# Weight maxima dealt 3, 2, 2, 1 and squares 2, 1, 1 over the first attention steps, and one root and one reciprocal for two batches in the last stage

## The chip, the cores and the metric

The kernel runs as one launch on one core of one Trainium2 chip. The metric is the device time of the launch in microseconds (us). Three timed runs of the kernel before gave 409.97, 409.61 and 407.93 us, so the median is 409.61 us. The engines are named as in the profile: PE is TensorE's matmul, PEld its weight load, DVE is VectorE, ACT is ScalarE, POOL is GpSimd, and SP is SyncE, which here only issues DMAs.

## What is computed

16 batches of 256 tokens with 128 channels go through a block with adaptive layer norm: causal linear attention with 16 heads of 8, then a mixture of 8 experts of which each token takes two. Cut to what matters here:

```python
h = _layernorm(x) * (1 + ca) + sa
x = x + ga * linear_attention(h)                 # cumulative sums of k (x) v, 16 heads
h = rmsnorm((_layernorm(x) * (1 + cb) + sb) @ W_in.T, in_norm_w)
gates = softmax over the two best of (h @ Wr.T + expert_bias)
for e in range(8):
    oe = (silu(h @ Wg[e].T) * (h @ Wu[e].T)) @ Wd[e].T
    out = out + gates[:, e:e + 1] * rmsnorm(oe, enorm_w[e])
x = x + gb * (rmsnorm(out, out_norm_w) @ W_out.T)
```

## The kernel before

A token sits on one of 128 partitions, and a batch is two tiles of 128 tokens. Every engine has its own program in a written order, and the engines meet only in semaphores. The kernel has three stages.

**Attention and routing** is a pipeline of steps. In step s one batch is normalized (`nrm`, batch s), the one before it is projected to q, k and v (`qkv`), and batches s-2 to s-5 are in the running state (`att`), the output projection (`prj`), the way into the experts (`inp`) and the routing (`rte`). Steps 0 to 7 are written out and use only the batches that exist: `inp` begins in step 4 and `rte` in step 5. Steps 8 and later are a loop. Between two steps nothing synchronizes all engines; each goes on as its waits allow. On DVE a step begins with `den` (L1130) and ends with `weights(s)`; on ACT a step ends with the deviation `sd2` of the second layer norm (L665), the squares of the routing and the second normalization `xn2`.

Work on the expert weights is put into these steps. They are loaded by SP early on: `wguT` (4 MB) into `late`, then `wd` (2 MB) and `enorm` (0.5 MB), the last two counted by `moe_ld`. Their scales have to be known before the expert stage. DVE takes the maximum of |wgu| in eight chunks of 1024 columns (`wmaxs`, L1089): two chunks at the end of each of steps 3, 4, 5 and 6, that is `MAX_STEPS`. At the end of step 6 it joins them (L1094 to L1097), and in step 7 (`SCALE_STEP`) the scale goes through PE and comes back (`weight_power`, `weight_scale`, L1108 to L1119). ACT takes sums of squares of `wd` in four chunks of 1024 columns (L739): two in step 6 and two in step 7, that is `SQUARE_STEPS`. In an ACT step they stand between the first normalization (`xn`, L631) and `sd2` (L665). DVE waits for `sd2` in `norm_inv` (L909), ahead of its `weights(s)`.

**The experts** are tiles of 256 rows of one expert each, paced by PE. The change does not touch them.

**The combination** mixes the two expert rows of every token, normalizes the mix, multiplies by `W_out` and adds x, a batch at a time. For a batch b: POOL makes `half` (L603); DVE adds the other half, `mix_experts` (L1422, two instructions); PE transposes the mix (L1872); ACT takes its sum of squares (`norm_out`, L867, two instructions), copies the transposed mix to `mixT` (L873) and takes the root `rms5` (L874); PE multiplies (L1880); DVE takes the reciprocal `rinv5` (`rms_out`, L1429) and writes the output `ob` (`add_out`, L1438, two instructions); SP stores it. On DVE the order of a turn is: reciprocal of batch b-2, mix of batch b, output of batch b-2. Batches 0 to 7 are written out, and their loads from DRAM come in the groups of `LOADS`, each with a root and coefficients of its own (L859, L1411, L1413). Batches 8 to 15 are a loop of two rounds with four batches each.

Of the kernel before, what the change touches and what calls it, by code (L numbers as in the profile page):

```python
# [100 lines left out]
def block_kernel(nc, x, c_wmod, weights_all, qkv_b, out_b, e_bias, wguT, wdT, e_norm, consts, place, filler, out):  # L101
    ctx = ExitStack()
    with ctx:
        def sb(name, shape, dt=F32):
            return ctx.enter_context(nc.sbuf_tensor(name, shape, dt))
# [164 lines left out]
        ob = kv[:, 0].rearrange("p t s -> p (t s)")[:, 0:4 * L].rearrange("p (j t d) -> p j t d", j=4, t=NT)  # L270
        mixT = mixT.rearrange("p j t d -> p j (t d)")
        rms4, rinv4, coef = (sb(n, [P, B * NT, K]) for n in ("rms4", "rinv4", "coef"))
        ssq4 = sb("ssq4", [P, 2, NT])
        rms5 = sb("rms5", [P, 2, NT])
        rinv5 = sb("rinv5", [P, 2, NT])

        bk = [ctx.enter_context(nc.psum_tensor(f"bank{i}", [P, 512], F32)) for i in range(8)]

# [343 lines left out]
        def _(act):  # L622
# [53 lines left out]
            def step(nrm, qkv, att, prj, inp, rte):  # L676
# [54 lines left out]
                    w = bass.ds(nrm[0] * WC - (SCALE_STEP + 1) * WC, WC)  # L731
                    nc.scalar.activation(w_hi[:, w], wgu[:, w], ACT.Copy, scale=w_by[:]).then_inc(whi_done, 1)
                s = nrm[0] if nrm is not None else B
                if isinstance(s, int) and s in SQUARE_STEPS:

                    if s == SQUARE_STEPS[0]:
                        act.wait_ge(moe_ld, 32)
                    for c in range(2 * (s - SQUARE_STEPS[0]), 2 * (s - SQUARE_STEPS[0]) + 2):
                        nc.scalar.activation(wd_junk, wd[:, c * DC:(c + 1) * DC], ACT.Square,  # L739
                                             accum_out=wd_sq[:, c:c + 1]).then_inc(wdsq_done, 1)  # L740
                        act.wait_ge(wdsq_done, c + 1)
# [117 lines left out]
                nc.scalar.activation(rms4[:, w], yb[:, w, :, D], ACT.Sqrt, bias=eps_rms[:],  # L859
                                     scale=1.0 / D).then_inc(rms4_done, 1)  # L860

            def norm_out(b, p, n):
                act.wait_ge(mix_done, b + 1)
                if again(n):
                    act.wait_ge(rinv5_done, b - 1)
                for t in range(NT):
                    nc.scalar.activation(junk[:], mix[:, p, t, :], ACT.Square,  # L867
                                         accum_out=ssq4[:, p, t:t + 1]).then_inc(ssq4_done, 1)
                    act.wait_ge(ssq4_done, NT * b + t + 1)
                act.wait_ge(mixT_ps, b + 1)  # L870
                if again(n):
                    act.wait_ge(o_ps, b - 1)
                nc.scalar.activation(mixT[:, p, :], bk[p][:, 0:L], ACT.Copy).then_inc(mixT_done, 1)  # L873
                nc.scalar.activation(rms5[:, p, :], ssq4[:, p, :], ACT.Sqrt, bias=eps_rms[:],  # L874
                                     scale=1.0 / D).then_inc(rms5_done, 1)

            rms_of_rows(0)
            rms_of_rows(1)
            for b in range(8):
                norm_out(*batch_of_turn(0, b))  # L880
                if b in (0, 1, 5):
                    rms_of_rows((0, 1, 5).index(b) + 2)
            with act.Fori(2, B // 4) as i:
                for j in range(4):
                    norm_out(*batch_of_turn(i, j))


        @block.vector
        def _(dve):
# [190 lines left out]

            def weights(s):

                if isinstance(s, int) and s in MAX_STEPS:

                    if s == MAX_STEPS[0]:
                        dve.wait_ge(wgu_ld, 16)
                    n = WN // len(MAX_STEPS)
                    for c in range((s - MAX_STEPS[0]) * n, (s - MAX_STEPS[0] + 1) * n):
                        nc.vector.tensor_reduce(wmaxs[:, c:c + 1], wgu[:, c * WC:(c + 1) * WC], AX.X, ALU.max,  # L1089
                                                apply_absolute_value=True).then_inc(wmaxs_done, 1)  # L1090
                    if s == MAX_STEPS[-1]:
# [324 lines left out]
            def mix_experts(b, p, n):  # L1416
                dve.wait_ge(half_done, b + 1)
                if again(n):
                    dve.wait_ge(mixT_ps, b - 1)
                    dve.wait_ge(ssq4_done, NT * (b - 1))  # L1420
                for t in range(NT):
                    last = nc.vector.scalar_tensor_tensor(  # L1422
                        mix[:, p, t, :], yb_of(b, t, 1), coef[:, bass.ds(b * NT + t, 1), 1],
                        half[:, p, t, :], ALU.mult, ALU.add)
                last.then_inc(mix_done, 1)

            def rms_out(b, p, n):
                dve.wait_ge(rms5_done, b + 1)
                nc.vector.reciprocal(rinv5[:, p, :], rms5[:, p, :]).then_inc(rinv5_done, 1)  # L1429

            def add_out(i, j):
                b, p, _ = batch_of_turn(i, j)
                dve.wait_ge(rinv5_done, b + 1)
                dve.wait_ge(o_ps, b + 1)
                if not (isinstance(b, int) and b < 4):
                    dve.wait_ge(stored[j % 4], 16 * (i + j // 4))
                for t in range(NT):
                    last = nc.vector.scalar_tensor_tensor(  # L1438
                        ob[:, j % 4, t, :], bk[2 + p][:, t * D:(t + 1) * D], rinv5[:, p, t:t + 1],
                        x_all[:, bass.ds(b * L + t * P, P)], ALU.mult, ALU.add)  # L1440
                last.then_inc(ob_done, 1)

# [498 lines left out]
```

## Time and profile before

| | |
|---|---|
| median of the timed runs | 409.61 us |
| all timed runs | 409.97, 409.61, 407.93 us |
| profiled execution, its own time | 404.05 us |
| profiled execution, span of the core | 402.2 us |
| busy share of the span | PE 94%, DVE 81%, ACT 73%, POOL 60% |
| steps 3 to 7 of the attention stage | 23.6 to 78.5 us |
| combination | 371 to 402 us |

The span is what the trace covers; the remaining 1.85 us of the execution's own time lie around it. Places in the trace are given as us from the start of the span.

### The profile page before, as it was taken

The numbers are of one execution on the slowest core, as the hardware profiler recorded it, in microseconds if no ns is written. First come the engines' busy times: TensorE is split into PE (matmuls) and PEld (weight loads), VectorE is DVE, ScalarE is ACT, GpSimd is POOL, SyncE is SP. The second block draws the span as 40 slices with busy tenths as digits, with TensorE's granted clock in tenths as the row PEclk, the third lists the DMA queues.
The fourth block names the chain that finished last, engine by engine and source line by source line (L and its number), as shares of the span: only waits on it lengthen the run. The fifth ranks groups of instructions, "written<-read, shape, count | busy, mean of one in ns | idle before, by whom it ended". The sixth has DMA issues, their size and how long they took to land.

```text
span 402.2 us, 13139 instructions
## 1 busy us (share of the span) xinstructions
PE 376.7 (94%) x3890; PEld 315.5 (78%) x3891; DVE 324.2 (81%) x1040; ACT 292.0 (73%) x817; POOL 239.7 (60%) x211
## 2 busy tenths in 40 slices
PE   8899998999999999999799999999999999999764
PEld 4788886888888888885379989999989899984443
DVE  5568998899999999886979878777878777871786
ACT  5455767877778888646478777878778778874685
POOL 0665587678888888875544545555555545553341
PEclk9999999999999999999999999999999999999999
DMA  7999973647464330011134332323232333213933
GB/s 223 365 358 405 315 238 113 225 132 221 145 200 168 131 131 26 29 48 39 48 69 59 70 68 58 76 55 71 61 79 53 61 70 60 60 42 111 356 100 91
DMA packets 47380, 52.60 MB, mean 131 GB/s; under 512 B 34675, under 2 KB 40710, under 8 KB 44518
## 3 DMA queue, kind: packets, MB, share of 16 engines
q1 hardware_dynamic: 42806, 42.84, 35.3%
q0 software_dynamic: 4544, 9.39, 7.8%
q8 instruction: 16, 0.26, 0.3%
q14 instruction: 14, 0.11, 0.1%
HBM read 35.73 MB, written 30.38 MB: 164 GB/s over the span
## 4 chain that ended last, share of the span: by engine, by line
PE 69%; DVE 10%; issue 6%; ACT 6%; DMA 5%; POOL 3%; DVEq 0%; SPq 0%; ACTq 0%; POOLq 0%
PE bank L1512 11%; PE bank L1784 9%; PE bank L1788 8%; PE bank L1787 8%; PE bank L1592 4%; PE bank L1803 4%; PE bank L1805 4%; PE bank L1804 4%; PE bank L1535 3%; DVE prod L992 2%; ACT junk L867 2%; DVE wmaxs L1089 1%; DMA dispatched<-filler 1%; PE bank L1649 1%; PE bank L1599 1%
## 5 line engine op out<-in xcount | busy, mean ns | idle before, releaser
L583 POOL DMA_INDIRECT expert_rows<-late,to_place x74 | 78.1, 1056 | 75.2 <-DVE late L1365 63.2
L1784 PE MATMUL bank<-late,w_hi 128*128 128x256 f16 x312 | 85.1, 273 | 1.9 <-issue 1.2
L532 POOL TENSOR_TENSOR kv<-kv,v 128x1024 f32<-128x1024 f32 x32 | 67.7, 2133 | 29.9 <-ACT kv L716 29.7
L1788 PE MATMUL bank<-late,w_lo 128*128 128x256 f16 x312 | 85.1, 273 | 0.0
L1787 PE MATMUL bank<-late,w_hi 128*128 128x256 f16 x312 | 85.1, 273 | 0.0
L1351 DVE SCALAR_TENSOR_TENSOR kv<-bank,uscale,kv 128x512 f32<-128x512 f32 x78 | 58.4, 750 | 26.6 <-ACT kv L801 23.2
L550 POOL DMA_INDIRECT dispatched<-rows,pos x60 | 63.8, 1063 | 23.2 <-issue 17.6
L1512 PE MATMUL bank<-cst,kv 128*128 128x128 f32 x576 | 73.5, 278 | 1.0 <-DVE den L1130 1.0
L1512 PEld LDWEIGHTS bank<-cst,kv 128*128 128x128 f32 x576 | 68.1, 192 | 1.5 <-issue 1.5
L801 ACT ACTIVATE kv<-bank,descale 128x512 f32<-128x512 f32 x78 | 53.5, 687 | 13.1 <-PE bank L1788 9.2
L807 ACT ACTIVATE kv<-kv 128x512 f16<-128x512 f32 x78 | 48.8, 626 | 17.5 <-DVE kv L1351 14.7
L1358 DVE TENSOR_TENSOR kv<-kv 128x512 f16<-128x512 f32 x78 | 54.5, 700 | 5.3 <-ACT kv L807 3.7
L1804 PE MATMUL bank<-late,kv 128*128 x304 | 52.9, 219 | 0.0
L1803 PE MATMUL bank<-late,kv 128*128 x304 | 52.9, 219 | 0.0
L1805 PE MATMUL bank<-late,kv 128*128 x304 | 52.9, 219 | 0.0
L992 DVE TENSOR_TENSOR prod<-bank,qT 128x384 f32<-128x384 f32 x96 | 49.6, 544 | 0.0
L1784 PEld LDWEIGHTS bank<-late,w_hi 128*128 x312 | 30.4, 98 | 6.7 <-issue 3.4
L1788 PEld LDWEIGHTS bank<-late,w_lo 128*128 x312 | 30.5, 98 | 3.7
L1787 PEld LDWEIGHTS bank<-late,w_hi 128*128 x312 | 30.5, 98 | 3.1
L1662 PE MATMUL bank<-ones 128*128 128x512 bf16 x129 | 29.5, 379 | 1.7 <-DMA dispatched<-rows,pos 1.7
L1804 PEld LDWEIGHTS bank<-late,kv 128*128 128x128 f16 x304 | 29.7, 98 | 0.4
L631 ACT ACTIVATE xn<-x_all,nmr,rs 128x128 f32<-128x128 f32 (+1 forms) x64 | 27.8, 482 | 3.0 <-DVE nmr L914 2.9
(248 smaller groups left out, 787.2 us busy)
## 6 DMA issues: line engine op xcount, KB each, us to landing
dispatched<-filler SPq DMA_DIRECT2D x17, 1032.0 KB
late<-wguT SPq DMA_DIRECT2D x1, 4096.0 KB, 18.0
late<-expert_rows SPq DMA_DIRECT2D x1, 2064.0 KB, 12.6
gates_bc<-gate_rows SPq DMA_DIRECT2D x1, 2048.0 KB, 7.2
wd<-wdT SPq DMA_DIRECT2D x1, 2048.0 KB, 25.2
out<-kv SPq DMA_DIRECT2D x16, 128.0 KB, 1.8
expert_rows<-late,to_place POOLq DMA_INDIRECT x78
late<-expert_rows SPq DMA_DIRECT2D x1, 1032.0 KB, 7.9
```

The costliest lines, as they stand in the source:

```text
L532: nc.gpsimd.tensor_tensor(kvt[:, 0:HD, :, :], k_in, v_in.to_broadcast([P, HD, H, HD]), ALU.mult).then_inc(kv_done[t], 1)
L550: pool.indirect_dma_start(hbuf, bass.IndirectOffsetOnAxis(ap=pos[:, p, t * K + k:t * K + k + 1], axis=0), rows[:, p, t, k, :], None).then_ ...
L583: pool.indirect_dma_start(ybuf, bass.IndirectOffsetOnAxis(ap=to_place[:, s, r:r + 1], axis=0), yt[:, s, r, :], None).then_inc(y_scat[s], 16)
L992: nc.vector.tensor_tensor(prod[:, t, cc * THIRD * P:(cc + 1) * THIRD * P].rearrange("p (e i) -> p e i", i=P), cum, qT[:, p, t * P:(t + 1) ...
L1351: nc.vector.scalar_tensor_tensor(gu[:, h, :], U[h], uscale[:], sg[:, h, :], ALU.mult, ALU.mult).then_inc(gu_done, 1)
L1512: last = mm(CUM[cc][:, j * P:(j + 1) * P], kv[:, p, t, e * D:(e + 1) * D], tri, start=True, stop=True)
L1784: mm(o, wh, hi, start=True, stop=False)
L1787: mm(o, wh, lo, start=False, stop=False)
L1788: last = mm(o, wl, hi, start=False, stop=True)
L1803: mm(o, gu_hi[:, s % 2, h, g], wh, start=(f == 0 and (apart or r == 0)), stop=False)
L1804: mm(o, gu_lo[:, s % 2, h, g], wh, start=False, stop=False)
L1805: last = mm(o, gu_hi[:, s % 2, h, g], wl, start=False, stop=(f == FC - 1 and (apart or r == RB - 1)))
```

## The change

Three tables of work are dealt anew.

- The eight chunks of the maxima (`MAX_CHUNKS`) go three to step 3, two to step 4, two to step 5 and one to step 6. Joining them stays at the end of step 6.
- The four chunks of the squares (`SQUARE_CHUNKS`) go two to step 4, one to step 6 and one to step 7. The wait for `moe_ld` goes with the first of them, to step 4.
- In the combination the sums of squares of two batches stand side by side (`ssq4`, `rms5` and `rinv5` have four batch slots), and ACT takes one root (L876 after the change) after the odd batch. DVE takes one reciprocal (L1431 after it) for both, and it stands behind the mix of the next even batch, no longer ahead of it. The two outputs that need it follow.

```diff
-        MAX_STEPS = range(SCALE_STEP - 4, SCALE_STEP)
+        MAX_CHUNKS = {SCALE_STEP - 4: range(0, 3), SCALE_STEP - 3: range(3, 5), SCALE_STEP - 2: range(5, 7),
+                      SCALE_STEP - 1: range(7, WN)}
-        SQUARE_STEPS = range(B - WN - DN // 2, B - WN)
+        SQUARE_CHUNKS = {SCALE_STEP - 3: range(0, 2), SCALE_STEP - 1: range(2, 3), SCALE_STEP: range(3, DN)}
...
-            def norm_out(b, p, n):
+            def norm_out(i, j):
...
                 nc.scalar.activation(mixT[:, p, :], bk[p][:, 0:L], ACT.Copy).then_inc(mixT_done, 1)
-                nc.scalar.activation(rms5[:, p, :], ssq4[:, p, :], ACT.Sqrt, bias=eps_rms[:],
-                                     scale=1.0 / D).then_inc(rms5_done, 1)
+                if j % 2:
+
+                    if again_turn(i):
+                        act.wait_ge(rinv5_done, 2 * i + j // 2 - 1)
+                    nc.scalar.activation(rms5[:, j - 1:j + 1, :], ssq4[:, j - 1:j + 1, :], ACT.Sqrt, bias=eps_rms[:],
+                                         scale=1.0 / D).then_inc(rms5_done, 1)
...
-            def rms_out(b, p, n):
-                dve.wait_ge(rms5_done, b + 1)
-                nc.vector.reciprocal(rinv5[:, p, :], rms5[:, p, :]).then_inc(rinv5_done, 1)
+            def rms_out(i, j):
+                pair, slots = 2 * i + j // 2, slice(j % 4, j % 4 + 2)
+                dve.wait_ge(rms5_done, pair + 1)
+                nc.vector.reciprocal(rinv5[:, slots, :], rms5[:, slots, :]).then_inc(rinv5_done, 1)
...
                 for j in batches:
-                    before = batch_of_turn(i, j - 2)
-                    rms_out(*before)
                     mix_experts(*batch_of_turn(i, j))
+                    if j % 2 == 0:
+                        rms_out(i, j - 2)
                     add_out(i, j - 2)
...
+            rms_out(0, B - 2)
             for b in (B - 2, B - 1):
-                rms_out(*batch_of_turn(0, b))
                 add_out(0, b)
```

On ACT, in step 4 of the attention stage, the program before has these rows (`q_raw`, `qT`: the query; `xn` is the first and `xn2` the second normalized input; `sd2` is what DVE waits for):

```order
L723 ACTIVATE q_raw<-bank3,small 128x256
L725 ACTIVATE qT<-q_raw,eps_f 128x256
L631 ACTIVATE xn<-x_all,nmr,rs 128x128 x2
L665 ACTIVATE sd2<-mv2,eps_ln 128x2
L670 ACTIVATE junk,ssq<-bank7 128x128 x2
```

The changed program has at the same place:

```order
L722 ACTIVATE q_raw<-bank3,small 128x256
L724 ACTIVATE qT<-q_raw,eps_f 128x256
L630 ACTIVATE xn<-x_all,nmr,rs 128x128 x2
L738 ACTIVATE w_lo,wd_sq<-wd 128x1024 x2
L664 ACTIVATE sd2<-mv2,eps_ln 128x2
L669 ACTIVATE junk,ssq<-bank7 128x128 x2
```

Two squares of `wd` now stand ahead of `sd2` in step 4. In step 6 and in step 7 one square stands there where two did.

On DVE, in the loop of the combination, a turn of an even batch reads before (`prod` is the mix, `kv` the output, `bank2` and `bank3` the products of the even and the odd batch, ISA and REGISTER_ALU are register work):

```order
L1429 RECIPROCAL rinv5<-rms5 128x2
L1417 REGISTER_ALU
L1422 ISA x2
L1422 SCALAR_TENSOR_TENSOR prod<-late,coef,prod 128x128
L1422 ISA x2
L1422 SCALAR_TENSOR_TENSOR prod<-late,coef,prod 128x128
L1436 REGISTER_ALU
L1438 ISA
L1438 SCALAR_TENSOR_TENSOR kv<-bank2,rinv5,x_all 128x128
L1438 ISA
L1438 SCALAR_TENSOR_TENSOR kv<-bank2,rinv5,x_all 128x128
```

In the changed program it reads:

```order
L1423 ISA x2
L1423 SCALAR_TENSOR_TENSOR prod<-late,coef,prod 128x128
L1423 ISA x2
L1423 SCALAR_TENSOR_TENSOR prod<-late,coef,prod 128x128
L1430 REGISTER_ALU
L1431 RECIPROCAL rinv5<-rms5 128x4
L1438 REGISTER_ALU
L1440 ISA
L1440 SCALAR_TENSOR_TENSOR kv<-bank2,rinv5,x_all 128x128
L1440 ISA
L1440 SCALAR_TENSOR_TENSOR kv<-bank2,rinv5,x_all 128x128
```

The reciprocal moved from ahead of the mix to between the mix and the first output that needs it, and it now covers four columns: it needs the root that ACT takes after the odd batch of the pair. The turn of an odd batch has no reciprocal any more.

## Rows read from the trace of the kernel before

**Rows 1.** The page: busy time by engine, and the chain by engine.

```profile
PE 376.7 (94%) x3890; PEld 315.5 (78%) x3891; DVE 324.2 (81%) x1040; ACT 292.0 (73%) x817; POOL 239.7 (60%) x211
...
PE 69%; DVE 10%; issue 6%; ACT 6%; DMA 5%; POOL 3%; DVEq 0%; SPq 0%; ACTq 0%; POOLq 0%
```

**Rows 2.** Steps 4, 6, 8: us, busy PE PEld DVE ACT POOL, clock, DMA share, GB/s.

```profile
33.88:43.80 9.92, 9.66 (x106) 8.58 (x105) 8.75 (x32) 6.57 (x20) 5.46 (x4) 1.00 1.01 397
...
54.64:67.28 12.64, 11.25 (x117) 9.37 (x115) 11.11 (x49) 9.58 (x27) 9.76 (x8) 1.00 0.47 153
...
78.47:88.80 10.33, 10.04 (x108) 8.42 (x107) 9.80 (x44) 8.33 (x24) 8.00 (x7) 1.00 0.43 133
```

**Rows 3.** Timeline of DVE, steps 4, 6 and 7: start, us, instruction, [idle before].

```profile
41.10 0.15 DVE L909 RECIPROCAL rs<-sd 128x2 f32<-128x2 f32 x1
...
41.55 2.33 DVE L1089 TENSOR_REDUCE wmaxs<-late 128x1 f32<-128x1024 f32 x2
...
63.77 0.17 DVE L909 RECIPROCAL rs<-sd 128x2 f32<-128x2 f32 x1 [0.76 <-ACT sd L665]
...
76.29 0.17 DVE L909 RECIPROCAL rs<-sd 128x2 f32<-128x2 f32 x1 [0.46 <-ACT sd L665]
...
77.69 0.16 DVE L1116 COPY wpow<-bank 128x1 f32<-128x1 f32 x1 [0.63 <-PE bank L1658]
```

**Rows 4.** Timeline of ACT, steps 4 and 6.

```profile
39.33 0.86 ACT L631 ACTIVATE xn<-x_all,nmr,rs 128x128 f32<-128x128 f32 x2
40.09 0.28 ACT L665 ACTIVATE sd<-mv,eps_ln 128x2 f32<-128x2 f32 x1
...
62.25 1.06 ACT L739 ACTIVATE w_lo<-wd 128x1024 f16<-128x1024 f32 x1
...
63.44 0.30 ACT L665 ACTIVATE sd<-mv,eps_ln 128x2 f32<-128x2 f32 x1
```

**Rows 5.** Timeline of SP: the issue of the load of `enorm`.

```profile
29.87 0.43 SPq L416 DMA_DIRECT2D enorm<-e_norm  x1
```

**Rows 6.** DMA issues: KB, and median us from issue to landing.

```profile
enorm<-e_norm SPq DMA_DIRECT2D x1, 512.0 KB, 10.0
```

**Rows 7.** Timeline of ACT in the combination: first root of loads, batches 8 to 12.

```profile
370.88 0.30 ACT L859 ACTIVATE rms<-late,eps_rms 128x4 f32<-128x4 f32 x1 [5.16 <-DMA late<-expert_rows]
...
388.44 0.29 ACT L874 ACTIVATE rms<-ssq,eps_rms 128x2 f32<-128x2 f32 x1
388.62 0.30 ACT L867 ACTIVATE junk<-prod 128x128 f32<-128x128 f32 x1
...
389.48 0.38 ACT L873 ACTIVATE prod<-bank 128x256 f32<-128x256 f32 x1
389.75 0.29 ACT L874 ACTIVATE rms<-ssq,eps_rms 128x2 f32<-128x2 f32 x1
...
392.40 0.29 ACT L874 ACTIVATE rms<-ssq,eps_rms 128x2 f32<-128x2 f32 x1
393.07 0.31 ACT L867 ACTIVATE junk<-prod 128x128 f32<-128x128 f32 x1 [0.39 <-DVE prod L1422]
```

**Rows 8.** Timeline of DVE in the combination.

```profile
371.28 0.18 DVE L1411 RECIPROCAL rinv<-rms 128x4 f32<-128x4 f32 x1 [7.96 <-ACT rms L859]
371.50 0.16 DVE L1413 TENSOR_TENSOR coef<-rinv,gate_all 128x4 f32<-128x4 f32 x1
...
384.00 0.35 DVE L1411 RECIPROCAL rinv<-rms 128x32 f32<-128x32 f32 x1 [0.29 <-ACT rms L859]
...
389.00 0.15 DVE L1429 RECIPROCAL rinv<-rms 128x2 f32<-128x2 f32 x1
389.20 0.62 DVE L1422 SCALAR_TENSOR_TENSOR prod<-late,coef,prod 128x128 f32<-128x128 f32 x2
389.79 0.61 DVE L1438 SCALAR_TENSOR_TENSOR kv<-bank,rinv,x_all 128x128 f32<-128x128 f32 x2
390.31 0.15 DVE L1429 RECIPROCAL rinv<-rms 128x2 f32<-128x2 f32 x1
```

More of the change, by code:

```diff
@@ L272, in block_kernel @@
         rms4, rinv4, coef = (sb(n, [P, B * NT, K]) for n in ("rms4", "rinv4", "coef"))
-        ssq4 = sb("ssq4", [P, 2, NT])
-        rms5 = sb("rms5", [P, 2, NT])
-        rinv5 = sb("rinv5", [P, 2, NT])
+        ssq4, rms5, rinv5 = (sb(n, [P, 4, NT]) for n in ("ssq4", "rms5", "rinv5"))
         bk = [ctx.enter_context(nc.psum_tensor(f"bank{i}", [P, 512], F32)) for i in range(8)]
@@ L733, in step @@
                 s = nrm[0] if nrm is not None else B
-                if isinstance(s, int) and s in SQUARE_STEPS:
-                    if s == SQUARE_STEPS[0]:
+                if isinstance(s, int) and s in SQUARE_CHUNKS:
+                    if SQUARE_CHUNKS[s][0] == 0:
                         act.wait_ge(moe_ld, 32)
-                    for c in range(2 * (s - SQUARE_STEPS[0]), 2 * (s - SQUARE_STEPS[0]) + 2):
+                    for c in SQUARE_CHUNKS[s]:
                         nc.scalar.activation(wd_junk, wd[:, c * DC:(c + 1) * DC], ACT.Square,
@@ L860, in rms_of_rows @@
                                      scale=1.0 / D).then_inc(rms4_done, 1)
-            def norm_out(b, p, n):
+            def norm_out(i, j):
+                b, p, n = batch_of_turn(i, j)
                 act.wait_ge(mix_done, b + 1)
-                if again(n):
-                    act.wait_ge(rinv5_done, b - 1)
                 for t in range(NT):
                     nc.scalar.activation(junk[:], mix[:, p, t, :], ACT.Square,
-                                         accum_out=ssq4[:, p, t:t + 1]).then_inc(ssq4_done, 1)
+                                         accum_out=ssq4[:, j, t:t + 1]).then_inc(ssq4_done, 1)
                     act.wait_ge(ssq4_done, NT * b + t + 1)
@@ L879, in _ @@
             for b in range(8):
-                norm_out(*batch_of_turn(0, b))
+                norm_out(b // 4, b % 4)
                 if b in (0, 1, 5):
@@ L884, in _ @@
                 for j in range(4):
-                    norm_out(*batch_of_turn(i, j))
+                    norm_out(i, j)
         @block.vector
@@ L1081, in weights @@
             def weights(s):
-                if isinstance(s, int) and s in MAX_STEPS:
-                    if s == MAX_STEPS[0]:
+                if isinstance(s, int) and s in MAX_CHUNKS:
+                    if MAX_CHUNKS[s][0] == 0:
                         dve.wait_ge(wgu_ld, 16)
-                    n = WN // len(MAX_STEPS)
-                    for c in range((s - MAX_STEPS[0]) * n, (s - MAX_STEPS[0] + 1) * n):
+                    for c in MAX_CHUNKS[s]:
                         nc.vector.tensor_reduce(wmaxs[:, c:c + 1], wgu[:, c * WC:(c + 1) * WC], AX.X, ALU.max,
                                                 apply_absolute_value=True).then_inc(wmaxs_done, 1)
-                    if s == MAX_STEPS[-1]:
+                    if MAX_CHUNKS[s][-1] == WN - 1:
                         dve.wait_ge(wmaxs_done, WN)
@@ L1425, in mix_experts @@
                 last.then_inc(mix_done, 1)
-            def rms_out(b, p, n):
-                dve.wait_ge(rms5_done, b + 1)
-                nc.vector.reciprocal(rinv5[:, p, :], rms5[:, p, :]).then_inc(rinv5_done, 1)
+            def rms_out(i, j):
+                pair, slots = 2 * i + j // 2, slice(j % 4, j % 4 + 2)
+                dve.wait_ge(rms5_done, pair + 1)
+                nc.vector.reciprocal(rinv5[:, slots, :], rms5[:, slots, :]).then_inc(rinv5_done, 1)
             def add_out(i, j):
                 b, p, _ = batch_of_turn(i, j)
-                dve.wait_ge(rinv5_done, b + 1)
+                dve.wait_ge(rinv5_done, 2 * i + j // 2 + 1)
                 dve.wait_ge(o_ps, b + 1)
@@ L1438, in add_out @@
                     last = nc.vector.scalar_tensor_tensor(
-                        ob[:, j % 4, t, :], bk[2 + p][:, t * D:(t + 1) * D], rinv5[:, p, t:t + 1],
+                        ob[:, j % 4, t, :], bk[2 + p][:, t * D:(t + 1) * D], rinv5[:, j % 4, t:t + 1],
                         x_all[:, bass.ds(b * L + t * P, P)], ALU.mult, ALU.add)
```

## The prediction

> **What bounds the kernel now.** I read the page first: PE is busy for 94% of the span and holds 69% of the chain that ended last [rows 1]. The change takes nothing from PE, so only the places where PE itself waits for DVE or ACT can move the time. Next I read the busy time by stretch, a step of the attention stage to each row. In the loop a step takes 10.33 us and PE is busy for 10.04 of it: there PE paces, and work on DVE or ACT is hidden. Step 6 takes 12.64 us with PE busy for 11.25 of it, so 1.4 us without work on PE, and with DVE busy for 11.11 [rows 2]. In the steps that carry the maxima DVE's end sets the next step's start: the next batch's statistics stand behind the maxima on DVE, then come ACT's `sd` and `hT`, then PE. Then the timelines of DVE and ACT, to see where DVE itself waits. In steps 6 and 7 it waits 0.76 and 0.46 us for ACT's `sd2`, in step 4 not at all [rows 3]. In the combination ACT works back to back, 1.32 us to a batch, and DVE 1.31 [rows 7, 8]: a stage in which two engines pass batches to and fro at nearly the same pace, with PE mostly idle. These two stretches are all that the change touches, and both lie on the path.
>
> **Maxima.** Two chunks take from 41.55 to the start of step 5 at 43.80, so one costs 1.13 us of DVE [rows 2, 3]. DVE has no idle time ahead of them in step 3, so the third chunk makes step 3 1.13 longer: **+1.1**. Steps 4 and 5 keep two. Step 6 loses one: **-1.1**, as long as something else doesn't end later there. What is left of step 6 is 12.64 - 1.13 - 0.76 (next part) = 10.75 us, still above the 10.33 at which PE paces a step, so the whole of it is given back. The maxima alone come to nothing.
>
> **Squares.** One square takes 1.19 us of ACT, from 62.25 to the `sd2` at 63.44 [rows 4]. In step 4 `sd2` starts at 40.09 right behind `xn`. With two squares between them it starts at 40.09 + 2.38 = 42.47, and DVE's reciprocal follows 0.33 later, as in step 6 (63.44 to 63.77): at 42.80. Before, it stood at 41.10 with no wait. DVE is late by **1.7 us** there [rows 3, 4]. Behind this wait on DVE are the shift of the norm, the two maxima and all of step 5, so nothing absorbs it: step 5 starts 1.7 later. The cover that the squares had in steps 6 and 7 was routing work on DVE, which in step 4 has not begun. In step 6 one square fewer brings `sd2` forward by 1.19, more than the wait of 0.76: **-0.8**. In step 7 the wait of 0.46 also goes, but DVE then waits 0.63 for PE at 77.69, and PE had been busy without a gap up to there [rows 3]: the scale comes when PE delivers it, so **0**. The loads: ACT now asks for `moe_ld` in step 4, at 40.1 + 1.1 = 41.2. `enorm`, the later of the two, is issued at 29.87 and lands 10.0 later, at 39.9 [rows 5, 6]. It is there, with 1.3 us to spare. The first stage sums to +1.1 - 1.1 + 1.7 - 0.8 = **+0.9**. Bounds: if the late `sd2` is wholly hidden, -0.8; if the gain in step 6 fails, +1.7.
>
> **Root and reciprocal.** A root takes 0.18 us of ACT's pace (388.44 to 388.62) and a reciprocal 0.1 to 0.2 of DVE's [rows 7, 8]. Eight of each go. Alone that would give ACT 0.18 per pair of batches. But the reciprocal for both batches needs the root after the odd one, and it now stands ahead of both outputs and of every later mix. DVE's loop becomes a ring, which I add up in instructions of this trace, from the root of an odd batch to that of the next. Root to reciprocal 0.40 (370.88 to 371.28); reciprocal to the output that reads it 0.22 (371.28 to 371.50); output to the next mix 0.52 (389.79 to 390.31) and 0.1 for the register work; the mix 0.62 (389.20); 0.1 to hand it to ACT (the 0.40 above less the root's own 0.30); squares 0.86 (388.62 to 389.48); copy 0.27 (to 389.75) [rows 7, 8]. That is 3.09 us for a pair. Before, it took 392.40 - 389.75 = 2.65 [rows 7]. The old ring held one batch: root, reciprocal, mix, squares and copy give 0.40 + 0.20 + 0.62 + 0.1 + 1.13 = 2.45 for two batches, just under ACT's 2.65, so it didn't show.
>
> How many pairs pay? The roots after batches 1 and 3 come before DVE asks for them, since the loads and halves pace that part. From batch 5 on: DVE asks for the root of pair (4, 5) ahead of coefficients 4 (384.00) [rows 8]; the ring makes these, and so the mix of batch 7, late by some 0.3. Pair (8, 9) comes by the ring plus the loop's entry, +0.1. Pair (10, 11) pays 3.09 - 2.65 = 0.45. At the loop's turn ACT waited 0.39 for DVE already [rows 7], so (12, 13) pays about 0.2. Pair (14, 15) pays 0.45 again. The sum is **+1.5**. Bounds: below, no wait at all and eight roots saved, 8 x 0.18 = -1.4; above, all seven passages from pair to pair pay 0.45, +3.1. I take 1.5, worked from the ring with the waits that the trace has.
>
> The rule weighed against this: the Trainium skill, "Perfetto Trace Analysis", section "Optimizing Scalar/DVE Operations", says that grouping small operations of Scalar and DVE helps when the engine is saturated. ACT is, in this loop, and by the rule alone the stage would gain the -1.4 of the lower bound. The same section says that breaking work up may let it complete sooner when the wait is elsewhere, and that is how I read the ring. The rule's gain is the first rival.
>
> **The sum.** +0.9 + 1.5 = +2.4 us on the profiled execution: 404.05 to 406.5. Its own time is 5.6 below the median of the timed runs; I carry the difference over, 409.61 + 2.4 = **412.0**.
>
> **The rivals.**
>
> 1. *Grouping pays* (15%): not slower. The place is the reciprocal behind the even mix. If ACT's root is there when DVE's mix ends, ACT paces and the stage loses 1.4; with +0.9 that is 409.1. It decides at the mix: its end would have to come 0.40 after the root's start or later. For it: DVE's own pace is 1.31 and it often comes late. Against: ACT starts the root at 389.75, DVE would be free at 389.79 and the root lands at 390.15 [rows 7, 8].
> 2. *The squares hide in step 4* (12%). DVE or PE is late there for another reason, and only -0.8 remains of the first stage: 409.6 - 0.8 + 1.5 = 410.3. Against it: DVE shows no wait at 41.10.
> 3. *Both of these* (5%): 409.6 - 0.8 - 1.4 = 407.4.
> 4. *The loads come late* (10%). If `enorm` lands beyond 41.2, each further us stands on ACT, then on DVE. Three us late is 1.7 more: 413.7. For it: the DMA engines are full in step 4 (share 1.01) [rows 2], and the timed runs take 5.6 us longer than this trace.
> 5. *The ring is shorter than I add it* (13%): hand-overs overlap, and the last stage costs 0.5: 411.0.
>
> **How the numbers follow.** The forecast has 45%, with a range of its own from 411.0 to 413.2. A measurement of this kernel tells about 0.5% from no change, 2.05 us, so slower begins at 411.66. Two thirds of the forecast lie there, and rival 4, and little of 5 and of the spread of the runs (the three before span 0.5%): 46%. Faster is rival 3 and the tail of 1: 7%. The rest, 47%, is within. The range from 408.9 to 413.9 leaves out rival 3 and the ends of 4 and of the spread.
>
> **What would show it.** In step 4 of the changed kernel DVE waits some 1.6 us for `sd2` at L909's place, in steps 6 and 7 not at all, and step 5 starts near 46.6 instead of 43.80. Step 3 is 1.1 longer, step 6 is 10.7 to 10.8. The loop from step 8 on is unchanged but starts 0.9 later. In the combination DVE waits 0.3 to 0.6 for the root at every even batch from 6 on, ACT waits for DVE at the odd batches, and two batches take 3.1. It is wrong if DVE's reciprocal never waits, if step 4 keeps 9.9 us, or if ACT stands at the first square for the load.

## The result and the profile after

The changed kernel takes 410.68 us (median of 9 runs, 409.20 to 412.01) against 409.61 for the kernel before (9 runs beside it, 406.57 to 411.55). The ratio is 1.0064, with a 95% interval of 1.0033 to 1.0096: 2.6 us slower, between 1.4 and 3.9. The two medians differ by only 1.07; the ratio compares runs taken side by side, so I go by it.

The page of the changed kernel, busy time by engine and the chain by engine (before: [rows 1]):

```profile
span 408.1 us, 13116 instructions
...
PE 379.5 (93%) x3890; PEld 317.7 (78%) x3891; DVE 323.7 (79%) x1032; ACT 291.4 (71%) x809; POOL 239.7 (59%) x211
...
PE 58%; DVE 18%; issue 8%; ACT 6%; DMA 4%; POOL 3%; DVEq 1%; SPq 0%; ACTq 0%; POOLq 0%
```

Eight instructions fewer on DVE and on ACT, as the change says, and their busy times are lower by 0.5 and 0.6. The chain runs over DVE for 18% of the span, where it was 10%. That is 33 us more, far beyond what the change costs, and the traces of its two halves below have 12% (e1) and 10% (e2): this share is no measure of the change.

The profiled span grew from 402.2 to 408.1, by 5.9, more than the timed runs did. I cut both traces at the same instructions (the `den` of each step; the first root of the loads in the combination; the end):

| stretch | before | after | difference |
|---|---|---|---|
| ahead of step 3 | 23.63 | 26.23 | +2.60 |
| step 3 | 10.25 | 11.38 | +1.13 |
| step 4 | 9.92 | 11.59 | +1.67 |
| step 5 | 10.84 | 10.85 | 0 |
| step 6 | 12.64 | 10.67 | -1.97 |
| step 7 | 11.19 | 11.18 | 0 |
| step 8 to the combination | 292.41 | 292.40 | 0 |
| combination | 31.32 | 33.80 | +2.48 |

The first row is no effect of the change, which has nothing there: over the traces of this study this stretch takes anything from 23.63 to 27.38, for kernels that are the same up to it. What lies in the parts that the change touches is +0.83 and +2.48, together 3.3, inside the interval. The stretch from step 8 to the combination, which it doesn't touch, takes from 291.94 to 293.03 over the same traces, so its agreement to 0.01 here is chance.

Busy time by stretch of the changed kernel, steps 4, 6 and 7 (columns as in [rows 2]):

```profile
37.61:49.20 11.59, 10.18 (x104) 8.67 (x104) 8.84 (x31) 8.76 (x24) 5.47 (x3) 1.00 0.84 311
...
60.05:70.72 10.67, 9.98 (x108) 8.35 (x107) 9.97 (x48) 8.43 (x25) 8.94 (x7) 1.00 0.40 129
70.72:81.90 11.18, 11.12 (x118) 9.55 (x117) 9.44 (x50) 8.43 (x25) 8.13 (x8) 1.00 0.62 199
```

Step 4 is longer by 1.67 with DVE as busy as before (8.84) and 1.4 us without work on PE. The clock is 1.00 in all of them.

Timeline of DVE, the same steps (before: [rows 3]), then of ACT in step 4 (before: [rows 4]):

```profile
46.50 0.17 DVE L911 RECIPROCAL rs<-sd 128x2 f32<-128x2 f32 x1 [1.58 <-ACT sd L664]
...
46.95 2.33 DVE L1090 TENSOR_REDUCE wmaxs<-late 128x1 f32<-128x1024 f32 x2
49.20 0.18 DVE L1131 TENSOR_SCALAR den<-bank 128x32 f32<-128x32 f32 x1
...
68.34 0.16 DVE L911 RECIPROCAL rs<-sd 128x2 f32<-128x2 f32 x1
...
69.01 1.21 DVE L1090 TENSOR_REDUCE wmaxs<-late 128x1 f32<-128x1024 f32 x1
...
79.19 0.14 DVE L911 RECIPROCAL rs<-sd 128x2 f32<-128x2 f32 x1
...
81.12 0.16 DVE L1117 COPY wpow<-bank 128x1 f32<-128x1 f32 x1 [1.18 <-PE bank L1660]
```

```profile
43.06 0.86 ACT L630 ACTIVATE xn<-x_all,nmr,rs 128x128 f32<-128x128 f32 x2
43.83 1.04 ACT L738 ACTIVATE w_lo<-wd 128x1024 f16<-128x1024 f32 x1
44.99 1.06 ACT L738 ACTIVATE w_lo<-wd 128x1024 f16<-128x1024 f32 x1
46.17 0.29 ACT L664 ACTIVATE sd<-mv,eps_ln 128x2 f32<-128x2 f32 x1
```

ACT goes from `xn` into the first square without a gap, so the loads had landed. `sd2` comes two squares later (46.17 - 43.83 = 2.34 us), DVE waits 1.58 for it, and the two maxima and step 5 stand behind that wait. In step 6 the wait of 0.76 is gone (68.34). In step 7 the wait for `sd2` (0.46) is gone too (79.19), and the one for PE grew from 0.63 to 1.18: the step stayed as long as it was.

Timeline of DVE in the combination (before: [rows 8]), then of ACT (before: [rows 7]). The first two rows of DVE lie ahead of the loop, the last two behind it:

```profile
387.56 0.18 DVE L1431 RECIPROCAL rinv<-rms 128x4 f32<-128x4 f32 x1 [0.40 <-ACT rms L876]
387.77 0.61 DVE L1440 SCALAR_TENSOR_TENSOR kv<-bank,rinv,x_all 128x128 f32<-128x128 f32 x2
...
393.56 0.81 DVE L1423 SCALAR_TENSOR_TENSOR prod<-late,coef,prod 128x128 f32<-128x128 f32 x2
394.58 0.18 DVE L1431 RECIPROCAL rinv<-rms 128x4 f32<-128x4 f32 x1 [0.20 <-ACT rms L876]
395.00 0.61 DVE L1440 SCALAR_TENSOR_TENSOR kv<-bank,rinv,x_all 128x128 f32<-128x128 f32 x2 [0.24 <-DVE rinv L1431]
395.59 0.62 DVE L1423 SCALAR_TENSOR_TENSOR prod<-late,coef,prod 128x128 f32<-128x128 f32 x2
...
404.17 0.18 DVE L1431 RECIPROCAL rinv<-rms 128x4 f32<-128x4 f32 x1 [0.98 <-ACT rms L876]
404.38 1.13 DVE L1440 SCALAR_TENSOR_TENSOR kv<-bank,rinv,x_all 128x128 f32<-128x128 f32 x4
```

```profile
378.58 0.31 ACT L858 ACTIVATE rms<-late,eps_rms 128x8 f32<-128x8 f32 x1 [0.40 <-DMA late<-expert_rows]
...
394.26 0.29 ACT L876 ACTIVATE rms<-ssq,eps_rms 128x4 f32<-128x4 f32 x1
...
396.25 0.31 ACT L865 ACTIVATE junk<-prod 128x128 f32<-128x128 f32 x1 [0.56 <-DVE prod L1423]
...
397.12 0.38 ACT L871 ACTIVATE prod<-bank 128x256 f32<-128x256 f32 x1
397.40 0.29 ACT L876 ACTIVATE rms<-ssq,eps_rms 128x4 f32<-128x4 f32 x1
```

This is the ring, a circle of instructions over both engines that each come only after the one before, so that a pair of batches can't take less than its length: root of batch 9 at 394.26, reciprocal 0.32 later, output 0.42 later, mix of batch 11 0.59 later, its squares on ACT 0.66 later (ACT waited 0.56 for them), copy 0.87 later, root of batch 11 0.28 later. The sum is 3.14 us for two batches, against 2.65 before.

The distance from each odd batch's root to the next shows where the 2.48 lies:

| roots of batches | 1 to 3 | 3 to 5 | 5 to 7 | 7 to 9 | 9 to 11 | 11 to 13 | 13 to 15 |
|---|---|---|---|---|---|---|---|
| before | 3.81 | 3.46 | 3.07 | 3.24 | 2.65 | 3.14 | 2.64 |
| after | 3.65 | 3.67 | 3.46 | 3.56 | 3.14 | 3.30 | 3.15 |

That is +0.05 up to batch 5 and +1.87 from there to batch 15. Ahead of batch 1 lie +0.33 (a load of rows came later, and ACT waited 0.40 for it at 378.58, where it had not waited before), behind batch 15 +0.23: four outputs now follow the last root instead of two.

### The profile page after: what moved, and what is told of

Read it like the earlier page. It is cut to its first block, busy times and chain, and to the rows that moved or that the text cites. A ratio compares the mean times of both kernels' runs of the same rounds, so it can differ in the third digit from the quotient of the medians.

```text
span 408.1 us, 13116 instructions
## 1 busy us (share of the span) xinstructions
PE 379.5 (93%) x3890; PEld 317.7 (78%) x3891; DVE 323.7 (79%) x1032; ACT 291.4 (71%) x809; POOL 239.7 (59%) x211
## 4 chain that ended last, share of the span: by engine, by line
PE 58%; DVE 18%; issue 8%; ACT 6%; DMA 4%; POOL 3%; DVEq 1%; SPq 0%; ACTq 0%; POOLq 0%
PE bank L1786 9%; PE bank L1790 8%; PE bank L1789 8%; PE bank L1514 7%; PE bank L1807 4%; PE bank L1805 4%; PE bank L1806 4%; DVE prod L994 4%; PE bank L1594 3%; PE bank L1537 2%; DVE wmaxs L1090 2%; DMA late<-expert_rows 1%; DVE st L899 1%; ACT junk L865 1%; DVE rows L1056 1%
## 5 line engine op out<-in xcount | busy, mean ns | idle before, releaser
L1514 PE MATMUL bank<-cst,kv 128*128 128x128 f32 x576 | 74.4, 280 | 1.1 <-DVE den L1131 1.1
L1514 PEld LDWEIGHTS bank<-cst,kv 128*128 128x128 f32 x576 | 69.1, 194 | 1.9 <-issue 1.7
```

The source lines that it names most:

```text
L1514: last = mm(CUM[cc][:, j * P:(j + 1) * P], kv[:, p, t, e * D:(e + 1) * D], tri, start=True, stop=True)
```

## The experiments

The theory to be tested is the prediction's, the ring theory for short: the squares in step 4 cost 1.7 and give 0.8 back, the maxima cost nothing, and in the combination the pair's reciprocal closes a ring of 3.1 us over both engines. Its main rival is that the combination loses for another reason than the pairing: by the place of the reciprocal behind the mix, or because DVE is full; for the first stage, that its +0.83 is only noise between executions. "Step sum" is steps 3 to 7, "gaps" the last row of the table above from 9 to 11 and from 13 to 15. One kernel's time and that of the kernel before stand side by side from the same chip; kernels without a ratio were run once.

**e1_front_only.** The two tables of the change, with the combination of before.

```diff
+MAX_CHUNKS = {SCALE_STEP - 4: range(0, 3), SCALE_STEP - 3: range(3, 5), SCALE_STEP - 2: range(5, 7), SCALE_STEP - 1: range(7, WN)}
+SQUARE_CHUNKS = {SCALE_STEP - 3: range(0, 2), SCALE_STEP - 1: range(2, 3), SCALE_STEP: range(3, DN)}
```

> Only the maxima 3, 2, 2, 1 and the squares 2, 1, 1; the combination is that of before. My theory (a square in step 4 makes DVE wait, the third chunk in step 3 is given back in step 6): step 3 takes 11.4 us, step 4 11.6 with a wait of 1.6 for sd2, step 5 10.85, step 6 10.7, step 7 11.2, together 0.8 to 0.9 more than before; the combination as before, roots of batches 9 to 11 and 13 to 15 2.65 us apart. Time: ratio to before 1.002. Rival (the whole loss of the changed kernel is here, through loads and DMAs that the steps disturb): ratio 1.006.

Measured: ratio 1.0019 (0.9980 to 1.0058), so +0.8 us with an interval from -0.8 to 2.4. The steps are 11.39, 11.59, 11.94, 10.67, 11.19; the combination is as before (31.34, gaps 2.65 and 2.64). All are those of the changed kernel but step 5, by 1.09. Busy time by stretch, steps 5 and 6 of this kernel, and one group of PE in step 5:

```profile
50.36:62.30 11.94, 11.06 (x102) 9.26 (x103) 10.57 (x46) 7.41 (x23) 6.10 (x4) 0.86 0.49 178
62.30:72.97 10.67, 10.21 (x112) 8.76 (x111) 9.97 (x48) 8.44 (x25) 8.65 (x7) 1.00 0.42 126
```

```profile
52.89 1.91 PE L1592 MATMUL bank<-small,hT 128*128 128x256 f32 x4
```

The granted clock was 0.86 over step 5 of this execution; the four matmuls of 1.91 take 1.13 at full clock in the trace of before. That 0.86 is a mean over the stretch, between the two levels of 2.4 and 1.2 GHz. I don't put it down to the tables: three kernels below with the tables of before had such a stretch (in step 7), and the changed kernel, with the same tables as e1, in no step. Without it the step sum is +0.85.

**e2_comb_only.** The combination of the change with the shares of before (maxima 2, 2, 2, 2; two squares in step 6, two in step 7).

```diff
+MAX_CHUNKS = {SCALE_STEP - 4: range(0, 2), SCALE_STEP - 3: range(2, 4), SCALE_STEP - 2: range(4, 6), SCALE_STEP - 1: range(6, WN)}
+SQUARE_CHUNKS = {SCALE_STEP - 1: range(0, 2), SCALE_STEP: range(2, DN)}
```

> Only the root and the reciprocal for two batches; maxima and squares are dealt as before. My theory (a ring over two batches: root, reciprocal, output, mix, squares, copy, root): roots of odd batches 3.1 us apart from batch 9 on, the first load root to the end of the span 1.5 to 2.0 us longer than before; steps 3 to 7 as before (54.8 us). Ratio 1.004 to 1.005. Rival (fewer small operations on the paced engine shorten the stage): roots 2.5 us apart, ratio 0.997.

Measured: ratio 1.0060 (1.0028 to 1.0093), +2.4 us. Steps as before (sum 54.86 against 54.84); combination 34.07, +2.75, gaps 3.14 and 3.14. The load came 0.52 later than before in this execution, and 2.23 remains, more than the 1.5 to 2.0 expected. The two halves of the change, +0.8 and +2.4, are 3.2 together against +2.6 for both, which agrees within the intervals. The ratio of e1 alone doesn't tell its +0.8 from nothing; by the steps the first stage is no noise, since they repeat in both traces to 0.02 us outside the stretch of the low clock.

**e7_squares_only** and **e8_maxima_only.** One table each, combination of before.

```diff
 e7: MAX_CHUNKS as in e2
+SQUARE_CHUNKS = {SCALE_STEP - 3: range(0, 2), SCALE_STEP - 1: range(2, 3), SCALE_STEP: range(3, DN)}
 e8: SQUARE_CHUNKS as in e2
+MAX_CHUNKS = {SCALE_STEP - 4: range(0, 3), SCALE_STEP - 3: range(3, 5), SCALE_STEP - 2: range(5, 7), SCALE_STEP - 1: range(7, WN)}
```

> Squares 2, 1, 1 as in the change, maxima two to a step, combination of before. My theory: step 4 takes 11.6 us (wait of 1.6 for sd2), step 6 11.9 (before 12.64), steps 3, 5 and 7 as before (10.25, 10.85, 11.2): +0.9 together. If the third chunk in step 3 were the costly part, the sum would be 0.

> Maxima 3, 2, 2, 1 as in the change, squares two in step 6 and two in step 7, combination of before. My theory: step 3 11.4 us, steps 4 and 5 as before, step 6 between 11.5 and 11.6 (12.64 less one chunk; its wait of 0.76 for sd2 stands ahead of the maxima and stays), step 7 11.2: sum 0. Rival (step 6 was held up by something else, so nothing is given back): +1.1.

Measured: e7 408.38 and e8 405.65, beside a kernel before of 406.91. By the steps, e7 has step 4 at 11.59 and step 6 at 11.79, step sum 55.69: +0.85. e8 has step 3 at 11.38 and step 6 at 11.60, sum 54.94: +0.10. Timeline of DVE, e7 in steps 4 and 6, then e8 in step 6:

```profile
44.77 0.17 DVE L910 RECIPROCAL rs<-sd 128x2 f32<-128x2 f32 x1 [1.59 <-ACT sd L666]
...
66.61 0.15 DVE L910 RECIPROCAL rs<-sd 128x2 f32<-128x2 f32 x1
```

```profile
66.20 0.17 DVE L910 RECIPROCAL rs<-sd 128x2 f32<-128x2 f32 x1 [0.85 <-ACT sd L666]
```

The whole loss of the first stage is the squares' wait in step 4; one square fewer in step 6 removes the wait there, and with the maxima alone it stays.

These two kernels also say how well the combination of before repeats. It takes 31.32, 31.34 and 31.36 in three traces (before, e1, e8), but 32.16 in e7, with gaps of 3.06 and 2.64: at one output of the loop DVE stood idle for 0.51 with nothing in the profile to wait for. So a single gap of one trace can be 0.4 off; the gaps of the new order count because they repeat, four times at 3.14 or 3.15 in the changed kernel and e2. Timeline of DVE, e7:

```profile
392.63 0.61 DVE L1438 SCALAR_TENSOR_TENSOR kv<-bank,rinv,x_all 128x128 f32<-128x128 f32 x2 [0.51 <-issue]
```

**e4_recip_ahead.** e2, with the pair's reciprocal ahead of the even batch's mix.

```diff
-                    mix_experts(*batch_of_turn(i, j))
                     if j % 2 == 0:
                         rms_out(i, j - 2)
+                    mix_experts(*batch_of_turn(i, j))
                     add_out(i, j - 2)
```

> As e2_comb_only, but the reciprocal of a pair stands ahead of the next even mix, where the single one stood before. My theory: the ring now holds both batches of the next pair in a row (root 0.40, reciprocal 0.20, mix 0.62, 0.1, then two batches of ACT at 1.13 each): roots of odd batches 3.5 to 3.7 us apart. Rival (the place behind the mix costs, so the old place is better): 2.6 us.

Measured: 409.98; combination 36.51, +5.2 against before, gaps 3.85 and 3.74, above the 3.5 to 3.7 expected. Timeline of DVE:

```profile
392.36 0.18 DVE L1431 RECIPROCAL rinv<-rms 128x4 f32<-128x4 f32 x1 [0.64 <-ACT rms L876]
392.80 0.62 DVE L1423 SCALAR_TENSOR_TENSOR prod<-late,coef,prod 128x128 f32<-128x128 f32 x2 [0.27 <-issue]
...
396.21 0.18 DVE L1431 RECIPROCAL rinv<-rms 128x4 f32<-128x4 f32 x1 [0.98 <-ACT rms L876]
```

With a mix more in the ring (about 0.6) the gap grows by 0.60 to 0.71. So the place behind the mix is the better of the two, and the length of the ring sets the time, as the ring theory has it. The expectation was too low because it led the ring through two batches of ACT (3.58); in the trace it runs over DVE, through both mixes and the output between them. The first two rows show one thing more: behind a wait for the root, the mix starts 0.44 after the reciprocal, though it doesn't read it.

**e3_two_mixes.** e2, with both mixes ahead of the reciprocal and both outputs behind it: the root is to have no one waiting.

```diff
                     mix_experts(*batch_of_turn(i, j))
-                    if j % 2 == 0:
-                        rms_out(i, j - 2)
-                    add_out(i, j - 2)
+                    if j % 2:
+                        rms_out(i, j - 3)
+                        add_out(i, j - 3)
+                        add_out(i, j - 2)
```

> As e2_comb_only, but on DVE both mixes of a pair stand ahead of the reciprocal, and both outputs behind it. My theory: the ring is broken, since the squares of the next pair no longer wait for the root; roots of odd batches 2.5 to 2.7 us apart, ratio 0.998 to 1.000. Rival (the cost of e2 is that of the order or of the wider operations themselves, not of the wait for the root): still 3.1 us, ratio 1.004.

Measured: ratio 1.0024 (0.9993 to 1.0056); combination 32.67, gaps 3.16 and 3.11 where I had expected 2.5 to 2.7. A miss in the loop. Up to the loop's first pair the order does what it was made for: from the root of batch 5 to that of batch 9 it takes 6.04 us, where e2 takes 7.02 and the kernel before 6.31. This is most of the 1.40 by which its combination is shorter than that of e2. Its step 7 was also 1.64 longer at a granted clock of 0.87, with tables as before. Timeline of DVE, then of POOL:

```profile
392.75 1.63 DVE L1423 SCALAR_TENSOR_TENSOR prod<-late,coef,prod 128x128 f32<-128x128 f32 x4
394.31 0.17 DVE L1431 RECIPROCAL rinv<-rms 128x4 f32<-128x4 f32 x1
394.72 1.13 DVE L1440 SCALAR_TENSOR_TENSOR kv<-bank,rinv,x_all 128x128 f32<-128x128 f32 x4 [0.24 <-DVE rinv L1431]
...
399.41 1.25 DVE L1423 SCALAR_TENSOR_TENSOR prod<-late,coef,prod 128x128 f32<-128x128 f32 x4
400.57 0.17 DVE L1431 RECIPROCAL rinv<-rms 128x4 f32<-128x4 f32 x1
```

```profile
393.63 0.62 POOL L602 TENSOR_TENSOR prod<-late,coef 128x256 f32 x1 [1.40 <-DVE prod L1423]
```

The wait for the root is gone, and DVE is now full: two mixes 1.56, reciprocal to output 0.41, outputs 1.13 add up to 3.10. Two of these are more than I had counted. The mixes take 1.56 where POOL forms its half meanwhile, and 1.16 where it doesn't (399.41 to 400.57). And from reciprocal to output it is 0.41 in the loop, where it is 0.21 outside (387.56 to 387.77 above). So the rival has a part in it: DVE has less to spare than the prediction gave it.

**e9_two_mixes_small_half.** e3, with POOL's half cut to 16 of 128 columns; the other 112 are left out, so this kernel computes less.

```diff
-nc.gpsimd.tensor_tensor(half[:, p], yb[:, bass.ds(b * NT, NT), 0, 0:D],
+nc.gpsimd.tensor_tensor(half[:, p, :, 0:16], yb[:, bass.ds(b * NT, NT), 0, 0:16],
...
```

> e3_two_mixes with POOL's product half cut to 16 of the 128 columns of each tile; the other 112 columns of it are left out, so this run times a smaller computation. In e3 two mixes in a row took 1.56 us when a POOL product ran beside the second (392.75 to 394.31) and 1.16 when none did (399.41 to 400.57). My theory (DVE's mix is slowed while POOL runs a tensor operation): all pairs of mixes take 1.2 us, roots of odd batches 2.65 to 2.8 us apart where e3 had 3.11 to 3.16. Rival (loop register work makes the difference): as e3, 3.1.

Measured: 409.02, with step 7 at 12.83 and a clock of 0.87; gaps 3.00 and 2.76 against 3.16 and 3.11 of e3 and an expected 2.65 to 2.8. Timeline of DVE, then of POOL:

```profile
394.04 1.33 DVE L1423 SCALAR_TENSOR_TENSOR prod<-late,coef,prod 128x128 f32<-128x128 f32 x4
395.29 0.17 DVE L1431 RECIPROCAL rinv<-rms 128x4 f32<-128x4 f32 x1
```

```profile
394.92 0.28 POOL L602 TENSOR_TENSOR prod<-late,coef 128x32 f32 x1 [1.90 <-DVE prod L1423]
```

With POOL's instruction at 0.28 instead of 0.62 the two mixes take 1.25 instead of 1.56. That the slowing comes from POOL is shown by this; that it is all of what e3 missed is not: the first gap is still 0.2 above.

**e10_singles_behind.** Before, with each single reciprocal behind the mix instead of ahead: the new order, without pairs.

```diff
-                    rms_out(*before)
                     mix_experts(*batch_of_turn(i, j))
+                    rms_out(*before)
                     add_out(i, j - 2)
```

> The kernel before with one edit: the reciprocal of each batch (still one root and one reciprocal a batch) stands behind the next mix, ahead of its output. My theory: no wait for a root appears, but in the loop the reciprocal no longer has a mix behind it and costs 0.4 instead of 0.2: two batches 2.9 to 3.1 us apart instead of 2.65. Rival (only the wait for the second root costs): 2.65.

Measured: 408.22; combination 33.08, gaps 2.96 and 2.97. Timeline of DVE:

```profile
392.35 0.62 DVE L1422 SCALAR_TENSOR_TENSOR prod<-late,coef,prod 128x128 f32<-128x128 f32 x2
392.88 0.16 DVE L1429 RECIPROCAL rinv<-rms 128x2 f32<-128x2 f32 x1
393.28 0.61 DVE L1438 SCALAR_TENSOR_TENSOR kv<-bank,rinv,x_all 128x128 f32<-128x128 f32 x2 [0.24 <-DVE rinv L1429]
```

The order alone, with two reciprocals to a pair of batches, costs 0.3: each reciprocal stands directly ahead of its reader, and from its start to the output 0.40 passes (0.31 at the batch after it). Before, the mix lay between the two, 0.20 or 0.10 behind the reciprocal (389.00 to 389.20 in [rows 8]). This corrects the ring theory: the order has a price of its own. It is no share of the 0.5 of the changed kernel, which has one such reciprocal to a pair and not two, and where e10 loses most, from batch 3 to 5 (+0.43) and 11 to 13 (+0.39), the changed kernel loses 0.21 and 0.16. In the changed kernel the place of the reciprocal enters as one term of the ring, 0.42 where I had 0.22.

**e5_lag3.** e2, with outputs three batches behind instead of two and the pair's reciprocal ahead of the odd mix, so that both the root's way and the reciprocal's lie under a mix.

```diff
+                    lead = isinstance(i, int) and 4 * i + j < 3
+                    if j % 2:
+                        rms_out(i, j - 3)
                     mix_experts(*batch_of_turn(i, j))
-                    if j % 2 == 0:
-                        rms_out(i, j - 2)
-                    add_out(i, j - 2)
+                    if not lead:
+                        add_out(i, j - 3)
...
+            add_out(0, B - 3)
```

> As e2_comb_only, but the outputs follow three batches behind the mixes instead of two, and the reciprocal of a pair stands ahead of the next odd mix. After e3 I count two causes: the ring through the root, and on DVE the 0.4 us between a reciprocal and the output right behind it in the loop, where the single reciprocal had a mix behind it and cost 0.2. Here neither should be left: the reciprocal has a mix behind it, and it is asked for only when the even batch of the next pair is being squared. By the rows of before DVE needs 0.59 + 0.52 + 0.20 + 0.59 + 0.65 = 2.55 us for a pair and ACT 1.14 + 1.32 = 2.46: roots of odd batches 2.5 to 2.6 us apart, ratio 0.998 to 1.000. If only the wider operations or the loop's register work cost: 3.1 us again, ratio 1.004.

Measured: ratio 0.9985 (0.9950 to 1.0021); combination 30.58, 0.74 less than before; gaps 2.91 and 2.56. Timeline of DVE:

```profile
394.89 0.62 DVE L1423 SCALAR_TENSOR_TENSOR prod<-late,coef,prod 128x128 f32<-128x128 f32 x2 [0.50 <-POOL prod L602]
...
397.46 0.81 DVE L1423 SCALAR_TENSOR_TENSOR prod<-late,coef,prod 128x128 f32<-128x128 f32 x2
```

No wait for the root is left in the loop. The gap of 2.56 is what the expectation added up for DVE (2.55), 0.08 under before. The gap of 2.91 was to be the same and is not; it holds a wait of 0.50 for POOL's half. Of the 0.74 some 0.19 is a load that came earlier than before; e6 and e11 below, with the same combination, are 0.60 and 0.62 ahead of before with their loads taken out, and this one 0.55. The run changes the lag and the pairing at once: how much the lag of three would give without pairs, no run shows. Its step 7 had the low clock, 0.86 over most of it:

```profile
68.90:81.45 12.55, 11.72 (x103) 9.49 (x104) 9.52 (x49) 9.48 (x27) 7.26 (x6) 0.86 0.53 186
```

**e6_lag3_squares_567** and **e11_lag3_squares_567_again.** The same kernel twice, on two chips: e5, with one square in step 5, one in 6, two in 7.

```diff
-SQUARE_CHUNKS = {SCALE_STEP - 1: range(0, 2), SCALE_STEP: range(2, DN)}
+SQUARE_CHUNKS = {SCALE_STEP - 2: range(0, 1), SCALE_STEP - 1: range(1, 2), SCALE_STEP: range(2, DN)}
```

> e5_lag3, maxima two to a step as before, and squares one in step 5, one in step 6, two in step 7. In step 5 ACT is free from 50.22 and DVE asks for sd2 at 51.39, so one square of 1.19 just fits: step 5 stays at 10.85 to 10.9 us with no wait or one under 0.1. Step 6 loses its wait: 11.9 instead of 12.64. Step 7 as before, 11.2. Together 0.7 to 0.8 us less than before, plus what e5 gives; ratio 0.996 to 0.999. If the squares of step 5 delay something else there: step 5 1 us longer and ratio 1.000.

> The kernel of e6 once more, for a second interval. By the profile's stretches it should be 0.8 us shorter in steps 3 to 7 and 0.4 to 0.8 in the combination: ratio 0.996 to 0.997. If these gains are given back elsewhere: 1.000.

Measured: against the kernel before 0.9980 (0.9950 to 1.0009) and 0.9936 (0.9904 to 0.9968). Busy time by stretch of e6, steps 5 and 6:

```profile
45.63:56.49 10.86, 10.66 (x114) 9.13 (x113) 10.48 (x46) 8.33 (x25) 6.06 (x5) 1.00 0.87 279
56.49:68.27 11.78, 11.10 (x117) 9.36 (x115) 11.01 (x48) 8.50 (x25) 9.73 (x8) 1.00 0.42 143
```

Step 5 takes the square for nothing (10.86 against 10.84), step 6 gives 0.86 back; the step sum is 54.00, 0.84 less than before, and the combination of e11 is 30.75. By the traces it is ahead of the changed kernel in both stages; the two were not timed side by side. It is ahead of the kernel before by 0.8 us by the first ratio and 2.6 by the second, and only the second is clear of one. The traces give 0.84 + 0.22 (e6) and 0.85 + 0.57 (e11), so part of the 2.6 is not accounted for.

## Why the prediction came out as it did

The forecast was 412.0 from a sum of +2.4 us; the ratio says +2.6, and the two traces +3.3, or 3.0 without the late load. Both mechanisms were there, the squares' wait and the ring. The first stage was sized right; the combination lost more than forecast, and one of its two causes was missing from the account. That +2.4 meets +2.6 so closely is luck: the interval goes from 1.4 to 3.9. By its steps:

- **Maxima, +1.1 and -1.1.** Step 3 is 1.13 longer; e8 gives 1.04 back in step 6. Right.
- **Squares, +1.7, -0.8, 0.** Measured +1.67 (a wait of 1.58, forecast "some 1.6"), and in e7 -0.85 in step 6. In step 7 nothing, and for the reason given: the wait went over to PE. First stage +0.83 for +0.9. Right. The loads didn't come late (rival 4), and nothing else hid the squares (rival 2).
- **The ring, 3.09 us a pair.** Measured 3.14 and 3.15, but two terms were off in opposite ways: root to reciprocal took 0.32, not 0.40, and reciprocal to output 0.42, not 0.22. The 0.22 I had taken from rows outside the loop, where it is 0.21 in the changed kernel as well; inside the loop it is twice that. The 0.1 for register work stood on no row; with it I had 0.62 from the output to the next mix, and it took 0.59. The sum came out partly by luck.
- **How many pairs pay, +1.5.** From batch 5 to 15 it was 0.39, 0.32, 0.49, 0.16, 0.51: 1.87. The entry of pair (8, 9) was mis-sized (0.32 for 0.1). Two terms were left out: the tail, +0.23, since the outputs of batch 14 no longer go ahead of the last root, and the load, +0.33, which differs from one execution to the next. The term was +2.48 in the trace where I had +1.5, +2.15 without the load. The sign that I gave, a wait of 0.3 to 0.6 for the root at every even batch from 6 on, came only in part: the waits are 0.40, 0, 0.20, 0 and 0.20. At batches 10 and 14 the mix ahead of the reciprocal had been slowed by 0.20, which hid as much of the wait, and at 8 and 12 DVE had waited 0.42 for ACT and 0.48 for POOL just before.
- **The cause given for it** was not the whole. I put the loss down to the wait for the pair's root alone. e10 has no pairs and loses 0.3 all the same, because the reciprocal lost its cover, the mix between it and its reader. The step "reciprocal to the output that reads it 0.22" hid this; with the 0.42 of the trace, 0.20 of the ring's 3.14 is the order's. How the 0.5 divides between the two beyond that is not shown: they lie on one ring, and e3, which takes the root's wait away, fills DVE by another way.
- **Grouping pays (rival 1)**, and behind it the rule of the Trainium skill, "Perfetto Trace Analysis", section "Optimizing Scalar/DVE Operations", that larger grouped operations help a saturated engine: not in this order. The trace of the changed kernel has ACT waiting 0.56 at the odd batch, so it isn't saturated once the ring is closed. In e5, where nobody waits for the pair's root, the same pairing goes with 0.74 us less, though a longer lag came with it. What decided was the rule's condition, a saturated engine: the new order took it away.
- **The loop from step 8 on** was to be unchanged: 292.40 against 292.41. It starts 0.83 later, for the 0.9 forecast, once the stretch ahead of step 3 is taken out.

## What to carry to other kernels

Merging two small instructions of different batches saves their overhead and lengthens the loop of dependences by the time between the two; add up that loop in instructions of the trace, with hand-overs taken from inside the loop, before counting the saving. In a loop whose addresses come from registers, a small instruction directly ahead of its reader mostly cost 0.31 to 0.45 us here (start to start), and 0.10 to 0.21 with another batch's work between the two; in code without registers it was 0.21 even directly ahead. Work on a side engine that is moved to an earlier step must find cover there: look at what the engine does next in that step, not at its busy share.

## What the runs showed that I had not expected

- **POOL beside DVE.** A mix of DVE takes 0.61 to 0.62 us alone, 0.81 where POOL's product ran beside it (393.56 above; the rows of POOL below), and two in a row 1.56 for 1.16; with POOL's instruction cut to 0.28 they take 1.25 (e9). The overlap at 393.56 is 0.40 (393.35 + 0.61 - 393.56), half of which DVE lost. The output at 395.00 runs beside POOL's next product for 0.25 and takes its usual 0.61. The Trainium skill, "SBUF — State Buffer", section "Who interferes with whom", says that an operation of DVE with both inputs in SBUF contends with GpSimd's reads; the mix is one, and the trace agrees; the output reads one of its two from PSUM.

Timeline of POOL of the changed kernel:

```profile
393.35 0.61 POOL L602 TENSOR_TENSOR prod<-late,coef 128x256 f32 x1 [1.38 <-DVE prod L1423]
394.64 0.61 POOL L602 TENSOR_TENSOR prod<-late,coef 128x256 f32 x1 [0.68 <-DVE prod L1423]
```

- **Between dependent instructions in the loop.** From a reciprocal to the output that reads it 0.42 passes in the loop and 0.21 in the part without registers, for the same two instructions. I think of the register work between them in the loop, since in e4 a mix that doesn't read the reciprocal follows it by 0.44 as well, and DVE's idle time there is put down to no other engine. No run takes the registers away, so this is not shown.
- **The clock of single steps.** In e1, e3, e5 and e9 the granted clock was 0.86 to 0.87 over one step (5, 7, 7 and 7) and 1.00 in the ones beside it, which cost 1.1 to 1.7 us. PE's work in the step before was the same as where it didn't fall: 10.18 us busy in step 4 of e1 and of the changed kernel, 11.24 in step 6 of e3 and 11.25 before. Why it fell stays open; it is of the size of the effects that the ratios are to tell, and one trace is not enough for them.
